# Output projection and second attention's projections as three products of split operands

## The chip, the cores and the metric

The kernel runs on one core of one Trainium2 chip. The metric is device microseconds of one execution; the median of several timed runs is quoted, and one further execution is profiled. Engines are named as in the profile: PE is TensorE's matrix products and PEld its weight loads, DVE is VectorE, ACT ScalarE, POOL GpSimd, SP SyncE. SPq and ACTq are the DMA issues of SyncE and ScalarE.

## The reference

A two-layer block on `x` of shape (8, 256, 512), fp32, cut to what matters here:

```
h   = causal depthwise conv of x (8 taps from cond, bias)
q, k, v = split(h @ qkv_w.T + qkv_b)                 # 16 heads of 32
a   = softmax(q k^T * scale + alibi bias, causal) v
x1  = x + (a @ out_w.T + out_b)                      # output projection
Q, K, V = einsum('oc,bct->bto', W, x1) for Wq, Wk, Wv  # 256 x 256 each, 16 heads of 16, 512 positions
y   = softmax((Q K^T / 4 + b) * m + (1 - m) * -1e30) V  # second attention, mask m = cond
out = x1 + ffn(y)                                    # gate, up, SiLU, down; weights rebuilt from control points
```

In the second attention the 256 rows of `x1` are the channels and the 512 columns are the positions.

## The kernel before, in words

Each engine has one program, written out by hand, with semaphores between them. Batch 0 is written separately, batches 1 to 6 are a loop, batch 7 stands behind the loop. The feed-forward of batch b - 1 runs inside batch b, and the first attention's projections and first scores of batch b + 1 run at the end of batch b. Batch 0 also rebuilds the down weights (gathered, split into a rounded high part and a low rest, and stored in DRAM) and the gate and up weights, eight chunks that GpSimd combines.

Within a batch TensorE goes through: exponent scores of the first attention and its value products (`values1`), the feed's first gate and up product, the output projection (L1101, eight products of 128x128x512 in the order of `PROJECTION`), the query and key projections of the second attention (L1112, eight products of 128x128x512), its values (L1120, eight of 128x128x256), then windows of score products (L1147) mixed with the feed, and 16 rounds of exponent scores (L1183) and value products (L1196).

VectorE divides each of four 256-column groups of the attention output by its row sums (reciprocal L838, product L840, result `o1`), then handles the feed's first gated product (L786) and its low rest (L790), then adds the projection to the residual, one 512-column half at a time (L849, result `x1`). ScalarE copies the projected queries out (L674); VectorE splits them (`split`, cast L770 and subtraction L772), multiplies the keys by the mask (L857), and splits those.

SyncE's queue is in order. After `x1_out` it stores `x1` in DRAM (L401), loads the residual of the feed's batch (L404), copies mask rows into the key stack (L432, four copies over all four groups), and then copies high and low parts into the query stack `q2` and key stack `k2`, group by group (`stacks2`, L425, twelve copies a group; the first score of a group waits for 192 counts, all twelve). Later come the next batch's residual and mask, and rows of maxima (`max_rows`, L332). `q2` and `k2` hold constant rows, written once in batch 0.

The output projection and the three projections of the second attention use plain fp32 operands. The scores and the down projection use operands bitcast to `float32r`; the down projection is already a sum of three such products, high by high, high by low and low by high (L1007, L1008, L1009).

Of the kernel before, what the change touches and what calls it, by code (L numbers as in the profile page):

```python
# [2 lines left out]

# [12 lines left out]
P = 128  # L16
# [27 lines left out]
ROWS2 = 64  # L44
# [76 lines left out]
def round_scores(k, i):  # L121
# [15 lines left out]
    "v2_ready": CT, "v2_out": CT, "aug_step": 3, "aug_high": 1, "aug_low": 1, "aug_rows": 64,  # L137
# [9 lines left out]
    "down_step": NT - 1, "sum_ready": LT, "sum_out": LT, "xr_loaded": 16, "out_stored": 16,  # L147
}
# [11 lines left out]
def block_program(nc, x_lanes, x_rows, taps, conv_b, qkv_wT, qk_b, v_b, out_wT, out_b, slopes, cond, w2T, att_b,  # L160
# [5 lines left out]
    key_dram = nc.dram_tensor("key_rows", (6, H1 * L), F32, kind="Internal").ap()  # L166
    alibi_dram = nc.dram_tensor("alibi_rows", (4, H1 * L), F32, kind="Internal").ap()
    with ExitStack() as ctx:
# [62 lines left out]

        halves = probs[:, 1].rearrange("p e n -> p (e n)")
# [29 lines left out]
        bias_loaded = sem("bias_loaded")  # L262
        big_loaded = sem("big_loaded")
        qk_loaded = [sem(f"qk_loaded{c}") for c in range(CT)]
# [37 lines left out]
        def _(sp):  # L302
# [57 lines left out]
            for i in range(2):  # L360
# [17 lines left out]
            stacks1(0)  # L378

# [9 lines left out]
            def batch(b, first=False, last=False):  # L389
# [51 lines left out]
                if not last:  # L441
# [4 lines left out]
                    wait("aug_rows", 64)  # L446
                    load_mask(cond[b])
# [125 lines left out]
        def _(act):  # L573
# [53 lines left out]
            def batch(b, first=False, last=False):  # L627
# [35 lines left out]
                if first:  # L663
                    for c in range(3, 5):
                        load_chunk(c)
# [814 lines left out]
```

## Time and profile before

| what | value |
|---|---|
| median of three timed runs | 1302.64 us |
| lowest, highest | 1294.46, 1304.24 us |
| the profiled execution | 1298.3 us |
| its span, first to last instruction | 1296.5 us |
| TensorE busy | 1192.3 us, 92% of the span |
| VectorE, ScalarE, GpSimd busy | 57%, 39%, 27% of the span |
| mean granted TensorE clock | 0.966 |

A busy share is an average over stages with different limits. Matrix products are pipelined and their modelled ends overlap, so the step of a chain of products is read from their starts. An fp32 product appears as two records, a `float32r` product as one.

### The profile page before, as it was taken

How to read it: one execution, taken by the hardware profiler on the slowest of the kernel's cores; microseconds unless marked ns; L12 is line 12 of the kernel's file. 1: busy time of each engine (PE TensorE's matmuls, PEld its weight loads, DVE VectorE, ACT ScalarE, POOL GpSimd, SP SyncE). 2: the span in 40 equal slices, each digit the busy share in tenths (PEclk: the TensorE clock that was granted, in tenths of full speed). 3: DMA queues.
4: the chain of work that ended last, by engine and by line, in shares of the span. 5: the costliest groups of instructions: out<-in, count | busy, mean ns of one | idle time of the engine just before them, and what ended most of it. 6: DMA issues, size and time to landing. Idle time of an engine off the chain costs nothing.

```text
span 1296.5 us, 20804 instructions
## 1 busy us (share of the span) xinstructions
PE 1192.3 (92%) x7400; PEld 682.4 (53%) x7400; DVE 743.9 (57%) x1173; ACT 501.4 (39%) x699; POOL 344.8 (27%) x201
## 2 busy tenths in 40 slices
PE   5685799999999999999999999999999999999988
PEld 4342245564555645565545645556455655556335
DVE  7666644558445773558535683557734684457812
ACT  1131244325532265224633256323643245322652
POOL 3283780092003800075000910047000830000000
PEclk9887679999999999999999999999999999999999
DMA  8989604382226704275134913267043732257024
GB/s 307 297 317 281 201 2 114 137 214 92 54 64 178 241 24 114 100 180 164 24 94 150 240 52 75 64 193 210 19 114 132 193 118 50 67 167 228 18 116 177
DMA packets 81057, 180.89 MB, mean 140 GB/s; under 512 B 14468, under 2 KB 54356, under 8 KB 71284
## 3 DMA queue, kind: packets, MB, share of 16 engines
q1 hardware_dynamic: 65104, 119.62, 33.2%
q10 hardware_dynamic: 14592, 55.86, 12.7%
q0 software_dynamic: 1280, 4.20, 0.9%
q8 instruction: 68, 1.11, 0.4%
q14 instruction: 13, 0.11, 0.0%
HBM read 106.41 MB, written 21.14 MB: 98 GB/s over the span
## 4 chain that ended last, share of the span: by engine, by line
PE 72%; DVE 8%; DMA 7%; POOL 5%; SPq 3%; issue 3%; ACT 2%; ACTq 0%; DVEq 0%; POOLq 0%
PE psum L1196 9%; PE psum L1147 8%; PE psum L967 8%; PE psum L1007 5%; PE psum L973 4%; PE psum L996 4%; PE psum L1009 4%; PE psum L1008 4%; PE psum L985 4%; PE psum L1101 4%; DVE max L868 4%; PE psum L1112 3%; PE psum L1183 3%; PE psum L1064 3%; SPq L425 3%
## 5 line engine op out<-in xcount | busy, mean ns | idle before, releaser
L868 DVE TENSOR_REDUCE max<-psum 128x1 f32<-128x512 f32 x512 | 326.2, 684 | 121.8 <-PE psum L1147 120.3
L705 ACT ACTIVATE probs<-psum 128x1024 f32<-128x1024 f32 x256 | 248.0, 1022 | 158.5 <-PE psum L1183 157.3
L1147 PE MATMUL psum<-k,q 52*128 52x512 f32 x512 | 198.1, 511 | 32.2 <-DMA k<-low 17.0
L555 POOL TENSOR_TENSOR h<-h_in,tap 128x1024 f32<-128x1024 f32 x7 | 13.3, 1897 | 611.9 <-DVE low L772 611.9
L1147 PEld LDWEIGHTS psum<-k,q 52*128 52x128 f32 x512 | 85.2, 194 | 160.3 <-DVE max L868 102.4
L1196 PE MATMUL psum<-probs,v 128*32 128x512 f32 x1024 | 140.7, 622 | 0.4 <-ACT probs L705 0.3
L1183 PE MATMUL psum<-q,k 54*128 54x512 f32 x512 | 113.8, 444 | 14.3 <-ACT probs L705 7.4
L565 POOL TENSOR_TENSOR h<-h,products 128x1024 f32<-128x1024 f32 x49 | 116.5, 2378 | 3.8
L1007 PE MATMUL psum<-stack 128*128 128x512 f32 x256 | 108.2, 423 | 0.0
L770 DVE CAST high<-low 128x1024 fp32r<-128x1024 f32 x32 | 24.9, 779 | 143.2 <-ACT low L586 115.4
L967 PE MATMUL psum<-h,qkv_w 128*128 128x256 f32 x448 | 103.5, 384 | 0.6 <-POOL h L565 0.6
L1008 PE MATMUL psum<-stack 128*128 128x512 f32 x256 | 100.7, 393 | 0.0
L1009 PE MATMUL psum<-stack 128*128 128x512 f32 x256 | 100.5, 393 | 0.0
L604 ACT ACTIVATE probs<-psum 128x512 f32<-128x512 f32 x64 | 38.2, 597 | 159.9 <-PE psum L996 159.9
L967 PEld LDWEIGHTS psum<-h,qkv_w 128*128 128x128 f32 x448 | 82.8, 190 | 28.5 <-issue 18.4
L562 POOL TENSOR_TENSOR products<-h_in,tap 128x1024 f32<-128x1024 f32 x49 | 93.2, 1903 | 3.3
L659 ACT ACTIVATE probs<-psum 128x768 f32<-128x768 f32 x64 | 48.9, 810 | 94.1 <-PE psum L1084 94.1
L838 DVE RECIPROCAL inv<-psum 128x256 f32<-128x256 f32 x32 | 56.2, 1758 | 46.3 <-PE psum L1064 45.5
L1183 PEld LDWEIGHTS psum<-q,k 54*128 54x128 f32 x512 | 53.9, 192 | 46.6 <-ACT probs L705 26.1
L973 PE MATMUL psum<-qkv_w,h 128*128 128x512 f32 x128 | 70.7, 674 | 2.7 <-issue 2.7
L996 PE MATMUL psum<-z,w_gate_up 64*128 64x256 f32 x512 | 68.3, 384 | 2.9 <-DVE stack L790 2.9
L815 DVE TENSOR_REDUCE max<-psum 128x2 f32<-128x256 f32 (+1 forms) x128 | 63.1, 552 | 13.5 <-PE psum L1035 12.8
(112 smaller groups left out, 1595.7 us busy)
## 6 DMA issues: line engine op xcount, KB each, us to landing
stack<-wd_sorted ACTq DMA_DIRECT2D x40, 1024.0 KB, 6.4
stack<-wd_sorted SPq DMA_DIRECT2D x24, 1024.0 KB, 6.9
stack<-high SPq DMA_DIRECT2D x128, 128.0 KB, 2.4
stack<-low SPq DMA_DIRECT2D x64, 128.0 KB, 2.4
q<-high SPq DMA_DIRECT2D x128, 64.0 KB, 4.0
k<-high SPq DMA_DIRECT2D x128, 64.0 KB, 4.1
h_in<-in_x_lanes SPq DMA_DIRECT2D x9, 512.0 KB, 4.0
x<-in_x_rows SPq DMA_DIRECT2D x8, 512.0 KB, 5.3
```

What stands on the lines that cost most here:

```text
L565: nc.gpsimd.tensor_tensor(h[:], h[:], products[:], ALU.add).then_inc(S["conv_step"], 1)
L705: nc.scalar.activation(probs[:, u // 2 % 2, u % 2 * 2:u % 2 * 2 + 2, :], psum[:, 2 + u % 2 * 2:4 + u % 2 * 2, :], ACT.Exp)\
L868: nc.vector.reduce_max(max2[:, g, e, i, t:t + 1], psum[:, bank, :], AX_X).then_inc(S["s2_max"], 1)
L967: last = nc.tensor.matmul(psum[:, o % 2, 0:L], qkv_w[:, c, o * P:(o + 1) * P], h[:, c, :], start=c == 0, stop=c == CT - 1)
L973: last = nc.tensor.matmul(psum[:, V1_BANKS[t], :], h[:, c, t * P:(t + 1) * P], qkv_w[:, c, 2 * D:3 * D], start=c == 0, stop=c == CT - 1)
L996: last = nc.tensor.matmul(psum[:, GU_BANK + g, u * L:(u + 1) * L], w_gu[rows, u, n, :], z[rows, n % 2, :], start=True, stop=True, skip_gro ...
L1007: nc.tensor.matmul(psum[:, SUM_BANK + s, :], r(inter_h[lhs]), r(w_h), start=n + g == 0, stop=False)
L1008: nc.tensor.matmul(psum[:, SUM_BANK + s, :], r(inter_h[lhs]), r(w_l), start=False, stop=False)
L1009: last = nc.tensor.matmul(psum[:, SUM_BANK + s, :], r(inter_l[lhs]), r(w_h), start=False, stop=n == NT - 1 and g == 1)
L1147: nc.tensor.matmul(psum[:, banks[s], :], r(q2[rows, g, i, t * P:(t + 1) * P]), r(k2[rows, g, i, :]), start=True, stop=True).then_inc(S["s2 ...
L1183: last = nc.tensor.matmul(psum[:, 2 + u % 2 * 2 + e, :], r(k2[rows, g, u % 2, kt * P:(kt + 1) * P]), r(q2[rows, g, u % 2, :]), start=True, ...
L1196: last = nc.tensor.matmul(psum[e * BLK:(e + 1) * BLK, 6, :], v2[:, t, head, :], probs[:, t % 2, e, :], start=t == 0, stop=t == CT - 1, ski ...
```

## The change

In batches 1 to 7 the output projection and the query, key and value projections become sums of three `float32r` products. For that, both sides are split into a rounded high part and a low rest.

- Weights: in batch 0 ScalarE makes the high parts of `out_w` and `w2` in `probs` and stores them in DRAM; VectorE subtracts them, so that `out_w` and `w2` then hold the low rests. Batch 0 itself still multiplies plain fp32. The plain weights first go from DRAM to DRAM and are loaded behind the first stacks.
- The high parts come back from DRAM in every batch but the last, for the next one: `out_w`'s (1 MB) into groups 0 and 1 of `q2` after 16 exponent scores, `w2`'s (0.75 MB) into groups 2 and 3 of `k2` after the last.
- `o1` is split group by group into `high`, `x1` half by half into groups 2 and 3 of `q2`.
- The constant and mask rows that this overwrites are written again in each batch, in two halves: groups 0 and 1 before `stacks2(0)`, groups 2 and 3 before `stacks2(2)`.
- The query and key projections are now ordered by `x1` half first, then query or key.

```diff
 # SyncE, start of the program
-            sp.dma_start(out_w[:], out_wT.rearrange("(c p) n -> p c n", p=P)).then_inc(big_loaded, 16)
-            sp.dma_start(w2[:].rearrange("p i c n -> p (i c) n"), w2T.rearrange("(m p) n -> p m n", p=P))\
-                .then_inc(big_loaded, 16)
+            sp.dma_start(plain_out, out_wT).then_inc(plain_copied, 16)
+            sp.dma_start(plain_w2, w2T).then_inc(plain_copied, 16)
...
             stacks1(0)
+            sp.wait_ge(plain_copied, 32)
+            sp.dma_start(out_w[:], plain_out.rearrange("(c p) n -> p c n", p=P)).then_inc(big_loaded, 16)
+            sp.dma_start(w2[:].rearrange("p i c n -> p (i c) n"), plain_w2.rearrange("(m p) n -> p m n", p=P))\
+                .then_inc(big_loaded, 16)
...
                 if not first:
                     wait("proj_ready", LT)
                     sp.dma_start(x_res, x1_dram[b - 1]).then_inc(S["xr_loaded"], 16)
+                    for e in range(2):
+                        row = e * ROWS2
+                        sp.dma_start(q2[row + ONE2:row + MAX2, 0:2, :, :].rearrange("p g i n -> p (g i n)"),
+                                     key_dram[2:6, 0:2 * 2 * D]).then_inc(S["refixed"], 16)
...
+                def mask_rows2(g):
+                    for e in range(2):
+                        for i, part in enumerate((aug_h, aug_f)):
+                            row = e * ROWS2 + ONE2 + 2 * i
+                            sp.dma_start(k2[row:row + 2, g:g + 2, :, :].rearrange("p g i n -> p (g i) n"),
+                                         part[:, None, :].broadcast_to([2, 4, D])).then_inc(S["aug_rows2" if g else "aug_rows"], 16)
...
                 wait("aug_low", 1)
-                for e in range(2):
-                    for i, part in enumerate((aug_h, aug_f)):
-                        row = e * ROWS2 + ONE2 + 2 * i
-                        sp.dma_start(k2[row:row + 2, :, :, :].rearrange("p g i n -> p (g i) n"),
-                                     part[:, None, :].broadcast_to([2, NG * 2, D])).then_inc(S["aug_rows"], 16)
+                mask_rows2(0)
                 for g in range(NG):
+                    if g == 2:
+                        wait("v2_ready", CT)
+                        if not first:
+                            for e in range(2):
+                                row = e * ROWS2
+                                sp.dma_start(q2[row + ONE2:row + MAX2, 2:4, :, :].rearrange("p g i n -> p (g i n)"),
+                                             key_dram[2:6, 0:2 * 2 * D]).then_inc(S["refixed2"], 16)
+                                sp.dma_start(k2[row + MAX2:row + END2, 2:4, :, :].rearrange("p g i n -> p (g i n)"),
+                                             key_dram[2:4, 0:2 * 2 * D]).then_inc(S["refixed2"], 16)
+                        mask_rows2(2)
                     stacks2(g)
...
                 for g in range(1, NG):
                     max_rows(b, g)
+                if first:
+                    sp.wait_ge(high_stored, 32)
                 if not last:
+                    wait("t2_ready", 2 * 2 * CT)
+                    sp.dma_start(out_high_flat, high_out).then_inc(S["out_high"], 16)
                     stacks1(b + 1)
                     wait("conv_step", 2 * TAPS)
                     sp.dma_start(h_in[:, :, TAPS - 1:], x_lanes[b + 1]).then_inc(S["x_loaded"], 16)
+                    wait("t2_ready", NP)
+                    sp.dma_start(w2_high_flat, high_w2).then_inc(S["w2_high"], 16)
 # ScalarE, batch 0, behind load_chunk(3) and (4)
+                    wait("pv1_ready", CT)
+                    act.wait_ge(big_loaded, 32)
+                    for made, plain in zip(made_high, (out_flat, w2_flat)):
+                        nc.scalar.activation(r(made), plain, ACT.Copy).then_inc(weights_high, 1)
+                    for i, store in enumerate((high_out, high_w2)):
+                        act.wait_ge(weights_high, i + 1)
+                        act.dma_start(store, made_high[i]).then_inc(high_stored, 16)
 # VectorE, batches 1 to 7, per group of o1 (x1 likewise per half: add, cast, subtract)
+                    nc.vector.tensor_tensor(inv1[:], psum[:, 6 + g % 2, 0:L], inv1[:], ALU.mult)\
+                        .then_inc(S["o1_made"], 1)
+                    dve.wait_ge(S["o1_made"], fed(b, "o1_made", g + 1))
+                    nc.vector.tensor_copy(r(o1_h[:, g, :]), inv1[:]).then_inc(S["o1_high"], 1)
+                    dve.wait_ge(S["o1_high"], fed(b, "o1_high", g + 1))
+                    nc.vector.tensor_tensor(r(o1_l[:, g, :]), inv1[:], o1_h[:, g, :], ALU.subtract)\
                         .then_inc(S["o1_out"], 1)
 # VectorE, batch 0, behind the key split
+                if first:
+                    wait("v2_ready", CT)
+                    for i, plain in enumerate((out_flat, w2_flat)):
+                        dve.wait_ge(weights_high, i + 1)
+                        nc.vector.tensor_tensor(r(plain), plain, made_high[i], ALU.subtract).then_inc(weights_low, 1)
 # TensorE
+            def three_terms(out, stat_h, stat_l, moving_h, moving_l, start, stop):
+                nc.tensor.matmul(out, r(stat_h), r(moving_h), start=start, stop=False, skip_group_check=True)
+                nc.tensor.matmul(out, r(stat_h), r(moving_l), start=False, stop=False, skip_group_check=True)
+                return nc.tensor.matmul(out, r(stat_l), r(moving_h), start=False, stop=stop, skip_group_check=True)
...
+                for t, i in product(range(LT), range(2)) if not first else ((0, 0), (1, 0), (0, 1), (1, 1)):
...
+                            last = three_terms(psum[:, banks[o], :], w2_h[:, i, t, rows], w2[:, i, t, rows],
+                                               x1_h[:, t, :], x1_l[:, t, :], t == 0, t == LT - 1)
...
                     if n == 0:
                         wait(f"stack2_{g}", 192)
-                        if g == 0:
-                            wait("aug_rows", 64)
+                        if g % 2 == 0:
+                            wait("aug_rows2" if g else "aug_rows", 64)
+                            if not first and g:
+                                pe.wait_ge(S["refixed2"], fed(b, "refixed2", 64))
+                            elif not first:
+                                pe.wait_ge(S["refixed"], fed(b, "refixed", 32))
```

## Rows read from the trace of the kernel before

**Rows 1.** The page's chain that ended last, shares by engine.

```profile
PE 72%; DVE 8%; DMA 7%; POOL 5%; SPq 3%; issue 3%; ACT 2%; ACTq 0%; DVEq 0%; POOLq 0%
```

**Rows 2.** That chain in order of time, batch 3: start us, us, what.

```profile
538.17 0.24 PE psum L1081 x2
...
550.12 6.88 PE psum L1112 x16
...
558.48 1.24 DVE low L772
...
564.02 2.33 DMA k<-low
```

**Rows 3.** TensorE's timeline at batch 3's first score: start, duration, line, idle before.

```profile
566.57 0.50 PE L1147 MATMUL psum<-k,q 52*128 52x512 f32 x2 [0.26 <-DMA k<-low]
```

**Rows 4.** Group by line on TensorE: shapes, count, busy us, mean ns, idle before.

```profile
L1120 PE MATMUL psum<-w,x 128*128 128x256 f32 x128 | 28.9, 379 | 0.0
```

**Rows 5.** TensorE's timeline in a down projection: second and last of its twelve products.

```profile
563.63 0.40 PE L1008 MATMUL psum<-stack 128*128 128x512 f32 x1
...
565.92 0.39 PE L1009 MATMUL psum<-stack 128*128 128x512 f32 x1
```

**Rows 6.** VectorE's timeline in batch 3, attention output to query split.

```profile
540.76 1.76 DVE L838 RECIPROCAL inv<-psum 128x256 f32<-128x256 f32 x1 [0.87 <-PE psum L1064]
...
543.08 1.76 DVE L838 RECIPROCAL inv<-psum 128x256 f32<-128x256 f32 x1
544.87 0.42 DVE L840 TENSOR_TENSOR o<-psum,inv 128x256 f32<-128x256 f32 x1
...
550.16 0.69 DVE L849 TENSOR_TENSOR x<-psum,x 128x512 f32<-128x512 f32 x1 [1.88 <-PE psum L1101]
554.29 0.69 DVE L770 CAST high<-low 128x1024 fp32r<-128x1024 f32 x1 [3.44 <-ACT low L674]
555.02 1.23 DVE L772 TENSOR_TENSOR low<-low,high 128x1024 f32<-128x1024 f32 x1
```

**Rows 7.** SyncE's queue in batch 3, `x1` store to the first group's stacks.

```profile
551.02 0.36 SPq L401 DMA_DIRECT2D x_scratch<-x  x1
551.58 0.35 SPq L404 DMA_DIRECT2D o<-x_scratch  x1
...
554.11 1.29 SPq L432 DMA_DIRECT2D k<-aug_f  x1
555.54 4.00 SPq L425 DMA_DIRECT2D q<-high  x4
...
563.38 1.22 SPq L425 DMA_DIRECT2D k<-low  x2
```

**Rows 8.** Timelines: SyncE's last issues of the first maxima rows; their first use.

```profile
594.94 1.30 SPq L332 DMA_DIRECT2D q<-max_l  x2
...
602.12 0.40 PE L1183 MATMUL psum<-q,k 54*128 54x512 f32 x2
```

**Rows 9.** SyncE queue's own waits: us in total, times, longest us.

```profile
SPq L321 <- DVE high L770: 75.1, 14, 9.0
```

**Rows 10.** The chain in order of time in batch 0.

```profile
49.00 10.52 DMA wd_natural<-w_gate_up
...
185.07 3.69 PE psum L967 x16
```

**Rows 11.** Busy time by window, two stretches of batch 0: last three, clock, DMA share, GB/s.

```profile
50.00:60.00 10.00, 8.65 (x32) 4.82 (x30) 5.62 (x11) 0.00 (x0) 0.20 (x1) 0.81 0.89 318
...
90.00:100.00 10.00, 10.00 (x25) 4.39 (x24) 3.69 (x5) 0.93 (x2) 6.76 (x8) 1.00 1.04 378
```

**Rows 12.** The same view, a stretch at the end of batch 2.

```profile
526.00:528.00 2.00, 2.00 (x3) 0.72 (x3) 0.00 (x0) 0.00 (x0) 0.00 (x0) 0.50 0.07 16
```

**Rows 13.** The chain in order of time, the same product in two batches.

```profile
524.60 5.13 PE psum L973 x8
...
974.91 3.44 PE psum L973 x8
```

More of the change, by code:

```diff
@@ L2 @@
 from contextlib import ExitStack
+from itertools import product
 import concourse.bass as bass
@@ L446, in batch @@
                     wait("aug_rows", 64)
+                    wait("aug_rows2", 64)
                     load_mask(cond[b])
@@ L704, in batch @@
                         act.wait_ge(S["inter_low"], fed(b, "inter_low", NT))
+                    if j == 0 and first:
+                        act.wait_ge(high_stored, 32)
+                        act.wait_ge(weights_low, 2)
                     nc.scalar.activation(probs[:, u // 2 % 2, u % 2 * 2:u % 2 * 2 + 2, :],
@@ L848, in batch @@
                     wait("proj_ready", t + 1)
+                    if first:
+                        nc.vector.tensor_tensor(x1[:, t, :], psum[:, t, :], x1[:, t, :], ALU.add)\
+                            .then_inc(S["x1_out"], 1)
+                        continue
                     nc.vector.tensor_tensor(x1[:, t, :], psum[:, t, :], x1[:, t, :], ALU.add)\
+                        .then_inc(S["x1_made"], 1)
+                    dve.wait_ge(S["x1_made"], fed(b, "x1_made", t + 1))
+                    nc.vector.tensor_copy(r(x1_h[:, t, :]), x1[:, t, :]).then_inc(S["x1_high"], 1)
+                    dve.wait_ge(S["x1_high"], fed(b, "x1_high", t + 1))
+                    nc.vector.tensor_tensor(r(x1_l[:, t, :]), x1[:, t, :], x1_h[:, t, :], ALU.subtract)\
                         .then_inc(S["x1_out"], 1)
@@ L1100, in batch @@
                         wait("o1_out", c + 1)
-                    last = nc.tensor.matmul(psum[:, t, :], o1[:, c, t * P:(t + 1) * P], out_w[:, c, :],
-                                            start=c == 0, stop=c == CT - 1, skip_group_check=True)
+                    rows = slice(t * P, (t + 1) * P)
+                    if first:
+                        last = nc.tensor.matmul(psum[:, t, :], o1[:, c, rows], out_w[:, c, :],
+                                                start=c == 0, stop=c == CT - 1, skip_group_check=True)
+                    else:
+                        last = three_terms(psum[:, t, :], o1_h[:, c, rows], o1_l[:, c, rows],
+                                           out_h[:, c, :], out_w[:, c, :], c == 0, c == CT - 1)
                     if c == CT - 1:
@@ L1106, in batch @@
                 wait("p1_out", H1 // 2)
-                for i, (banks, ready) in enumerate(((Q2_BANKS, "q2_ready"), (K2_BANKS, "k2_ready"))):
-                    for t in range(LT):
-                        if i == 0:
-                            wait("x1_out", t + 1)
-                        for o in range(LT):
-                            last = nc.tensor.matmul(psum[:, banks[o], :], w2[:, i, t, o * P:(o + 1) * P],
-                                                    x1[:, t, :], start=t == 0, stop=t == LT - 1, skip_group_check=True)
-                            if t == LT - 1:
-                                last.then_inc(S[ready], 1)
+                if not first:
+                    pe.wait_ge(S["w2_high"], fed(b, "w2_high", 16))
+                for t, i in product(range(LT), range(2)) if not first else ((0, 0), (1, 0), (0, 1), (1, 1)):
+                    banks, ready = ((Q2_BANKS, "q2_ready"), (K2_BANKS, "k2_ready"))[i]
+                    if i == 0:
+                        wait("x1_out", t + 1)
+                    for o in range(LT):
+                        rows = slice(o * P, (o + 1) * P)
+                        if first:
+                            last = nc.tensor.matmul(psum[:, banks[o], :], w2[:, i, t, rows], x1[:, t, :],
+                                                    start=t == 0, stop=t == LT - 1, skip_group_check=True)
+                        else:
+                            last = three_terms(psum[:, banks[o], :], w2_h[:, i, t, rows], w2[:, i, t, rows],
+                                               x1_h[:, t, :], x1_l[:, t, :], t == 0, t == LT - 1)
+                        if t == LT - 1:
+                            last.then_inc(S[ready], 1)
                 for n in range(CT):
```

37 lines of the change are left out of this document (32 added, 5 removed).

## The prediction

> **What bounds the kernel now.** I read three views in turn. First the shares of the chain that ended last: TensorE holds 72% of it, VectorE 8%, DMA 7%, SyncE's queue 3% [rows 1]. So most microseconds taken from TensorE shorten the kernel, provided nothing else waits at the same place. Second, the chain in order of time around the changed stage of one steady batch (batch 3, 536 to 570 us; the other loop batches repeat it). TensorE's projections come first, then a VectorE split, then SyncE's copies, and the last link is 2.33 us of a copy into the key stack, landing at 566.34 [rows 2]. Third, the timeline shows the first score of the second attention starting at 566.57, after only 0.26 us idle on that copy [rows 3]. Thus two chains arrive together there: TensorE's own work, and the path x1, split, SyncE, stack. A shorter TensorE alone gains a quarter of a microsecond per batch. From that score on TensorE has hardly a gap to the batch's end, so the start of that score is what I compute. The change acts in batches 1 to 7; batch 0 only prepares weights.
>
> **TensorE's part.** One true fp32 product 128x128x512 is two records; 16 records take 6.88 us for the query and key projections [rows 2], 0.86 us a product. The split product already in the kernel, the down projection, runs from 563.63 to 565.92 in ten steps [rows 5], 0.229 us a step; three make 0.69 us. The output projection and query/key have 8 products each: 16 x 0.17 = 2.7 us saved. The values have 8 products of 256 columns: now 128 records for 8 batches, 28.9 us [rows 4], 3.6 us a batch; two consecutive split steps of 256 columns take 0.24 us [rows 2], so 24 x 0.12 = 2.9 us, 0.7 saved. In all 3.4 us a batch, 24 us in seven, if nothing else were paced.
>
> **VectorE's part, on the path.** Each 256-column group of the attention output now costs a reciprocal (1.76) and a product (0.42) [rows 6]. Added are a cast to the high part and a subtraction. The cast of 1024 columns takes 0.69 and the subtraction of 1024 takes 1.23 [rows 6]; scaled with a start of about 0.15 us (estimate from the product of 256 at 0.42 and the add of 512 at 0.69), 256 columns take about 0.28 and 0.41. Group 2's reciprocal starts at 540.76 [rows 6] because TensorE delivers then. Groups 2 and 3 then take about 3.0 each instead of 2.25, so group 3 is finished at 546.8 rather than 545.3. TensorE, faster now, gets to that group about 0.6 us before and waits. Behind it on VectorE are queued the feed's gated product and remainder, with a ScalarE cast between them, about 2.1 us: 549.0. Then x1 is made twice: add 0.69, cast 0.42, subtract 0.69 with gaps, 1.87 each. x1_out's first count is due at 550.85, the second at 552.7. Before, the second add ended at 550.85 [rows 6]. **x1 is 1.9 us later**, though its projection was shortened. TensorE idles some 1.2 us before the second projections, which then end about 0.5 us earlier than now; it would arrive at the first score near 565.3.
>
> The query split is 1.8 us later too: TensorE's 18 steps from 550.9 and a fill end at 555.4, and with ScalarE's copy the cast starts at 556.1 instead of 554.29 [rows 6]. The key products queue behind it on VectorE: the key's low part is ready near 561.5, against 558.48 + 1.24 = 559.72 [rows 2]. The new order of the query and key loops recovers nothing here, as the query's second half now stands behind the key's first.
>
> **SyncE's part, on the path.** SyncE's queue stores x1 at 551.02, loads the residual, issues four mask-row copies, then the stacks. The fourth mask copy takes 1.29 us, the first four query copies 4.00, against 1.22 for two afterwards [rows 7]: the four end at 559.54, so with two free issues of 0.61 at their end the queue is held up until about 558.3, 7.2 us behind the x1 store's issue. With x1 1.9 later the same queue starts at 552.9, and two constant-row copies are added before the masks; these are halved in bytes, not in number. Bounds for the first score. Below: no hold-up at all, query copies from 556.9, twelve issues of about 0.62 us and the same landing give 566.1, that is minus 0.3 (VectorE's parts allow it). Above: the hold-up shifts with x1 and two issues move from inside it to behind it, 1.9 + 1.1 = plus 3.0. I take plus 1.8, since the hold-up in these rows stands at a fixed distance from the x1 store.
>
> The Trainium skill (DMA: Bandwidth & Descriptors, "Why a DMA increments its semaphore by 16 and not by 1") says that a copy is spread over as many DMA engines as divide its outermost dimension. By it, two-partition mask rows use two engines, and halving them would shorten the hold-up; as an estimate by that page the shift would be nearer 1.3 us and the total near 1316. The slow fourth mask issue agrees with slow draining, but cannot tell which engines drained.
>
> The other eight added issues (constant rows and mask rows of groups 2 and 3) precede the stacks of those groups and push SyncE's later work by roughly 4 us with the shift above. Who waits: the first group's maxima rows, whose last issue pair ends at 594.94 + 1.30 = 596.24, needed by TensorE at 602.12 [rows 8]. Nearly all of that cover goes; I take 0, with up to 2 us a batch if it is short. The two streams of high weights follow quiet places in SyncE's queue: it waits 75.1 us over 14 waits for VectorE's casts at the first stacks [rows 9]. I take 0; without that cover one issue costs about 0.35 [rows 7]. The added semaphore waits on TensorE protect buffers freed long before, except the x1 and stack waits already counted.
>
> **Batch 0.** Its chain runs through DMA: a 1 MB store from 49.00 takes 10.52 us on it, and after further loads and GpSimd's convolution TensorE's work on the next batch enters it at 185.07 [rows 10]. DMA share is 0.89 at 318 GB/s and 1.04 at 378 GB/s in two stretches of it [rows 11]. The change adds a second load of 1.84 MB behind the first stacks (5.8 us at 318) and a store of the same size from ScalarE's queue (4.9 at 378). Before these sit two casts of about 1.9 and 1.4 us on ScalarE, and two subtractions on VectorE, about 4.3 or more, ahead of its sorts; TensorE's scores wait for both engines. Bounds: 2 us (the casts, if the copies fill holes) to 14 (all in sequence). I take 8, as the shares show few holes.
>
> **Sum.** Seven batches at 1.8 = 12.6, plus 8 = 20.6. The profiled execution took 1298.3 us (span 1296.5), so 1318.9. The median is 1302.64, 4.3 higher; the three timed runs lie on both sides of the profiled one. I say 1320.
>
> **Rivals.** (B) The clock falls as well. TensorE would wait some 2.5 to 3 us at the first score. In this trace the granted clock was 0.50 in 526 to 528, after a stretch in which TensorE had short waits [rows 12]; that is the 1.2 GHz level, full is 2.4. Eight records there took 5.13 us, and 3.44 in the like place of a later batch [rows 13], so 1.7 us. Once per batch: 12 more, 1331. Against it: no row shows a fall at the first score, where the wait now is 0.26 us [rows 3]. The Trainium skill (TensorE: Matmul & The Clock Gate, Part 1) likewise has two clock states and a fall after idleness.
>
> (C) Not slower: SyncE's hold-up is set by the data of the mask rows, not by x1. Then the first score comes 0.3 to 1.0 us earlier, the latter being TensorE's own arrival; seven batches give minus 2 to 7, batch 0 adds 2 to 8: 1293 to 1304, say 1300. It decides if the query copies start without a pause after the cast. For it: the slow issues are the fourth mask copy and those right behind it [rows 7]. Against: VectorE's order leaves the key's low part 1.8 us later anyway.
>
> (D) Faster: VectorE's added parts hide, and TensorE's 3.4 us come through in full: 1298.3 - 24 + 2 = 1276. For it: 72% of the chain [rows 1]. Against: VectorE is in order and runs group 2 and 3 back to back [rows 6]. That the change doesn't speed TensorE at all (three split products as long as one) would add to A only where TensorE is last, so it stays within A's range.
>
> **How the numbers follow.** A 0.52, B 0.17, C 0.21, D 0.10. The range 1296 to 1340 takes in A's bounds but for the last few microseconds of their worst sum (12.6 replaced by 21, 8 by 14, giving 1333, and 1340 with a late maxima row), B, and most of C; D stays out. Within 1%, about what a measurement of this kernel can tell from no change, is 1289.6 to 1315.7: most of C and a third of A. Faster takes D and a little of C.
>
> **What would show it.** In the profile after: split products at 0.23 us a step; x1's store 1.5 to 2 us later against the start of the output projection; TensorE idle 2 us or more before the first score with the key copy as releaser; batch 0's first TensorE work on the next batch near 193 instead of 185. Wrong if that idle time is under 0.5 us, or if the query copies follow the cast with no held issue.

## The result, and the profile after

The changed kernel took 1318.93 us (median of 4 runs, 1316.87 to 1319.84) against 1302.52 us of the kernel before beside it: a ratio of 1.0121, 95% interval 1.0088 to 1.0154. Timed once more, it took 1313.95 us, ratio 1.0088 (1.0055 to 1.0121). The change makes the kernel about 1% slower, 11 to 16 us. The profiled span is 1318.0 us, 21.5 us longer than before, with a mean granted clock of 0.953 against 0.966.

The page's chain of the changed kernel, shares by engine, answers to [rows 1]: TensorE fell from 72% to 56%, VectorE doubled, SyncE's queue went from 3% to 11%.

```profile
PE 56%; DVE 16%; SPq 11%; DMA 7%; issue 4%; ACT 3%; ACTq 1%; POOL 1%; DVEq 0%; POOLq 0%
```

Now the changed stage of batch 3. TensorE's timeline (start, duration, line, idle before in brackets):

```profile
564.16 0.50 PE L1044 MATMUL psum<-q,high 128*128 128x512 f32 x1 [0.70 <-DVE high L906]
...
567.91 0.50 PE L1044 MATMUL psum<-q,k 128*128 128x512 f32 x1 [0.73 <-DVE q L924]
...
573.55 0.28 PE L1044 MATMUL psum<-k,q 128*128 128x256 f32 x1
573.67 0.28 PE L1045 MATMUL psum<-w,q 128*128 128x256 f32 x1
...
584.11 0.50 PE L1254 MATMUL psum<-k,q 52*128 52x512 f32 x2 [1.65 <-DMA k<-low]
```

The 24 query and key products run from 567.91 to 573.55, 5.64 us where the fp32 ones took 6.88 [rows 2]; a value step is 0.12 us. By its steps TensorE does save the 3.4 us, and the brackets show where they went: 0.70 us of waiting for o1's low part, 0.73 for x1's, and 1.65 at the first score, where 0.26 stood before [rows 3].

VectorE's timeline of the same batch, beside [rows 6]:

```profile
561.10 1.76 DVE L895 RECIPROCAL inv<-psum 128x256 f32<-128x256 f32 x1
562.89 0.42 DVE L901 TENSOR_TENSOR inv<-psum,inv 128x256 f32<-128x256 f32 x1
563.35 0.29 DVE L904 CAST high<-inv 128x256 fp32r<-128x256 f32 x1
563.68 0.43 DVE L906 TENSOR_TENSOR high<-inv,high 128x256 fp32r<-128x256 f32 x1
...
568.95 0.69 DVE L924 TENSOR_TENSOR q<-x,q 128x512 fp32r<-128x512 f32 x1
573.07 0.69 DVE L827 CAST high<-low 128x1024 fp32r<-128x1024 f32 x1 [3.43 <-ACT low L728]
```

To compare batches I count from the transpose that turns the first attention's maxima (524.32 before, 541.50 after). The last group of o1 is finished 22.61 us behind it instead of 20.97, x1 28.14 instead of 26.53, the query cast starts 31.57 instead of 29.97: everything on VectorE is 1.6 us later. Then SyncE's queue, beside [rows 7]:

```profile
569.84 0.36 SPq L424 DMA_DIRECT2D x_scratch<-x  x1
...
573.89 0.62 SPq L459 DMA_DIRECT2D k<-aug_f  x1
574.64 2.46 SPq L452 DMA_DIRECT2D q<-high  x4
...
580.95 1.22 SPq L452 DMA_DIRECT2D k<-low  x2
```

The fourth mask copy takes 0.62 us instead of 1.29 and the first four query copies 2.46 instead of 4.00: **the hold-up is gone**, though the copies still start 0.9 us behind the end of the cast, because SyncE is issuing mask rows until then. So SyncE gives back what VectorE lost, and the first score stands 42.61 us behind the transpose instead of 42.25.

The first maxima rows still come in time, with less to spare: their last issues end at 616.95, and TensorE uses them at 619.62, 2.7 us later, where 5.9 us lay between before [rows 8].

```profile
615.64 1.31 SPq L352 DMA_DIRECT2D q<-max_l  x2
...
619.62 0.41 PE L1290 MATMUL psum<-q,k 54*128 54x512 f32 x2
```

Where, then, are the 21.5 us? TensorE's timeline gives the opening of each batch. Batch 0's transpose is 3.0 us later, batch 0 itself is 9.95 us longer (170.98 against 161.03), and batches 1 to 7 are 8.6 us longer in all, +0.65, +3.59, +0.31, +0.90, -1.23, +4.77 and -0.40. The loop's loss is thus in two batches, 2 and 6, not in each. About 1.7 us of batch 6 only changed places: the clock fell at the opening of batch 5 before and at that of batch 6 after, which is also batch 5's -1.23. In batches 2 and 6, TensorE waited for down weights. The first line is from its list of waits (total us, times, longest), the next two are the waits of batch 2 in its timeline, and then come SyncE's issues of the two streams of high weights in that batch.

```profile
PE psum L1092 <- DMA stack<-wd_sorted: 3.8, 5, 1.1
...
455.97 0.50 PE L1092 MATMUL psum<-stack 128*128 128x512 f32 x1 [1.07 <-DMA stack<-wd_sorted]
...
461.44 0.50 PE L1092 MATMUL psum<-stack 128*128 128x512 f32 x1 [0.75 <-DMA stack<-wd_sorted]
...
502.39 0.35 SPq L508 DMA_DIRECT2D q<-high_out  x1
...
529.82 0.55 SPq L513 DMA_DIRECT2D k<-high_w  x1
```

The view by windows (after the busy times: clock, DMA share, GB/s) has the same stretch of batch 2, 51.35 us behind the transpose, in the kernel before:

```profile
426.41:446.41 20.00, 20.00 (x128) 14.03 (x127) 13.98 (x25) 4.78 (x9) 19.08 (x10) 1.00 0.97 304
```

and in the changed kernel, with the fall of the clock behind it:

```profile
440.00:460.00 20.00, 18.93 (x124) 13.20 (x122) 12.68 (x22) 4.22 (x9) 18.70 (x9) 1.00 0.99 274
...
476.00:478.00 2.00, 1.92 (x12) 0.34 (x9) 2.00 (x4) 1.94 (x2) 0.00 (x0) 0.75 0.05 13
478.00:480.00 2.00, 2.00 (x10) 1.15 (x7) 0.70 (x2) 0.02 (x1) 0.00 (x0) 0.50 0.04 8
```

The DMA engines are full from 440 to 460, but they were so before (0.99 and 0.97), and no weights came late then. Now two weight loads come 1.07 and 0.75 us late, and some 15 us later the clock is at 0.50, the 1.2 GHz level that [rows 12] showed at another place. Batch 6 repeats it (0.80 and 0.77 us, then the clock). The streams of high weights are issued some 40 us after these waits, and those of the batch before some 75 us ahead of them, so they do not bring them on. What does is not shown.

In batch 0 the chain in order of time now goes through ScalarE's queue and VectorE's subtractions and reaches the next batch's first product at 198.24 instead of 185.07 [rows 10]:

```profile
93.40 4.23 ACTq L695
97.73 3.29 ACT probs L716 x2
101.03 3.27 ACTq L719
104.33 4.91 ACTq L719
...
117.55 3.35 DVE out_w L940
120.90 2.20 DVE w L940
...
198.24 3.46 PE psum L1052 x16
```

### The profile page after: what moved, and what is told of

Its sections match the earlier page's. It is cut to its first block, busy times and chain, and to the rows that moved or that the text cites. A ratio compares the mean times of both kernels' runs of the same rounds, so it can differ in the third digit from the quotient of the medians.

```text
span 1318.0 us, 21393 instructions
## 1 busy us (share of the span) xinstructions
PE 1181.7 (90%) x7568; PEld 703.7 (53%) x7568; DVE 783.0 (59%) x1259; ACT 505.3 (38%) x701; POOL 347.3 (26%) x201
## 4 chain that ended last, share of the span: by engine, by line
PE 56%; DVE 16%; SPq 11%; DMA 7%; issue 4%; ACT 3%; ACTq 1%; POOL 1%; DVEq 0%; POOLq 0%
PE psum L1303 9%; PE psum L1052 8%; PE psum L1254 8%; SPq L452 7%; PE psum L1058 4%; DVE max L948 4%; PE psum L1092 4%; PE psum L1290 3%; DVE inv L895 3%; PE psum L1070 3%; PE psum L1093 3%; PE psum L1094 3%; PE psum L1081 2%; DMA stack<-wd_sorted 2%; SPq L459 2%
## 5 line engine op out<-in xcount | busy, mean ns | idle before, releaser
L1092 PE MATMUL psum<-stack 128*128 128x512 f32 x256 | 107.8, 421 | 3.8 <-DMA stack<-wd_sorted 3.8
L658 ACT ACTIVATE stack<-psum 128x512 fp32r<-128x512 f32 x64 | 38.3, 599 | 88.7 <-DVE psum L843 78.4
```

Source lines behind the costliest of these rows:

```text
L1092: nc.tensor.matmul(psum[:, SUM_BANK + s, :], r(inter_h[lhs]), r(w_h), start=n + g == 0, stop=False)
```

## The experiments

Theory: (1) in the loop, SyncE's in-order issues behind x1 set the first score, and VectorE's splits of o1 and x1 push x1 back; (2) in batch 0, making the high weights costs 8 us or more. The way of the plain weights, first from DRAM to DRAM and then loaded late, is called the detour. Rivals: the loss is all in batch 0, or all in the number of added copies. Each run was timed against the kernel before on the same chip. One profile is one draw: batch 0 of the changed kernel took 170.98 us in one and 163.77 in another. So verdicts go by the ratios, and the profiles by what repeats in each batch.

| run | median us | ratio | 95% interval | batch 1 opens | mean first score, batches 1 to 6 | mean from there to the batch's end |
|---|---|---|---|---|---|---|
| before | 1302.52 | 1 | | 226.40 | 41.66 | 107.84 |
| after | 1318.93 | 1.0121 | 1.0088 to 1.0154 | 239.34 | 41.98 | 109.03 |
| after, again | 1313.95 | 1.0088 | 1.0055 to 1.0121 | 232.55 | 41.92 | 109.21 |
| weights only | 1308.97 | 1.0034 | 1.0009 to 1.0058 | 237.47 | 42.12 | 108.83 |
| no weights | 1314.32 | 1.0069 | 1.0045 to 1.0093 | 234.92 | 42.18 | 109.81 |
| detour only | 1306.41 | 1.0033 | 1.0017 to 1.0049 | 234.20 | 41.57 | 108.38 |
| masks halved | 1303.04 | 0.9997 | 0.9970 to 1.0025 | 225.20 | 41.80 | 108.10 |
| SyncE's order | 1312.26 | 1.0062 | 1.0036 to 1.0089 | 234.48 | 41.03 | 109.40 |
| two queues | 1302.75 | 0.9997 | 0.9975 to 1.0018 | 233.47 | 40.41 | 110.02 |
| QKV only | 1301.39 | 0.9983 | 0.9960 to 1.0007 | 233.91 | 40.34 | 108.82 |
| output only | 1306.76 | 1.0013 | 0.9988 to 1.0038 | 234.37 | 42.36 | 108.28 |
| output, no split | 1304.00 | 1.0014 | 0.9991 to 1.0037 | 232.53 | 41.26 | 108.30 |
| QKV, two queues | 1296.68 | 0.9963 | 0.9937 to 0.9989 | 235.57 | 39.69 | 109.14 |
| QKV, late weights | 1298.46 | 0.9958 | 0.9931 to 0.9986 | 233.90 | 39.93 | 108.95 |

The last three columns come from TensorE's timeline of the profiled run: the transpose that opens batch 1; the first score's start, counted from its batch's transpose; and the time from there to the next transpose. In every profile at least one of the six batches takes 107.76 to 107.99 us for that last stretch, so about 107.8 is what it takes undisturbed, and what lies above is waits and clock. The profiled runs of after, weights only, no weights, detour only, output only and QKV, late weights are the slowest of their series, so their columns are high. The first score's place carries the clock too: where the clock fell at a batch's opening (batches 3 to 5 of the kernel before) it comes about 1.2 us later. Between batches with the same clock, after differs from before by 0.3 to 0.4 us, and QKV only by -0.8 to -1.0.

**Batch 0: weights only, no weights, detour only.** Three runs take batch 0's work apart. The first adds to the kernel before all of the change's weight preparation, and multiplies as before. The second takes casts, stores and subtractions out of the changed kernel (the weights are then not split: plain weights stand as both parts). The third adds to the kernel before only the detour.

```diff
 # detour only, on the kernel before
-            sp.dma_start(out_w[:], out_wT...).then_inc(big_loaded, 16)
-            sp.dma_start(w2[:]..., w2T...).then_inc(big_loaded, 16)
+            sp.dma_start(plain_out, out_wT).then_inc(plain_copied, 16)
+            sp.dma_start(plain_w2, w2T).then_inc(plain_copied, 16)
...
             stacks1(0)
+            sp.wait_ge(plain_copied, 32)
+            sp.dma_start(out_w[:], plain_out...).then_inc(big_loaded, 16)
+            sp.dma_start(w2[:]..., plain_w2...).then_inc(big_loaded, 16)
```

> The kernel before with batch 0's preparation alone: detour and late load of the weights, casts, stores of the high parts, subtractions. Later batches multiply plain fp32 with the low rests, so their output is left out of account; their work is that of before. Theory (batch 0 carries most of the loss): batch 0 grows by 13 us, as in the changed kernel (there batch 1's turn of the maxima comes at 239.3 instead of 226.4), later batches stay, total 1302.5 + 13 = 1315. Rival (the preparation is hidden and the later batches lose the time): at most 4 us more, 1302 to 1306.

> The changed kernel without casts, stores and subtractions in batch 0; the detour and late load stay, and the per-batch streams carry the plain weights, so the products are wrong by that and their work is the same. Theory: the turn of batch 0's maxima stays 3 us late (detour), the other 10 us of batch 0 go, total 1319 - 10 = 1309. Rival (the detour and late load alone delay batch 0's loads): no more than 3 us less, 1316 to 1319.

> The kernel before with nothing of the change but the way of the plain weights: copied from DRAM to DRAM at the start and loaded behind the first stacks; no casts, stores or subtractions. Theory (the copy and the late load are batch 0's cost, since all kernels with them open batch 1 at 232.5 to 239 us and the two without at 225 and 226): 1307 to 1310 us, batch 1 opens at 232 or later. Rival (the casts, held stores and subtractions are the cost): 1302 to 1305 us, batch 1 opens at 228 or earlier.

The preparation in all costs 0.34%, 4.4 us, between theory and rival. The detour alone costs 0.33%, the same, at 1306.41 us just below the range that I gave its theory and above the rival's; batch 1 opens at 234.20, as the theory had it. So casts, stores and subtractions add nothing measurable to the kernel before; the intervals would show some 4 us. Taking them out of the changed kernel gives 0.52% or 0.19%, by which of its two timings one takes; the intervals overlap with both, so for that kernel 0 to about 7 us stay open. How the detour costs 4 us is suggested by the chain of its profile, batch 0:

```profile
90.91 20.54 DMA z_table<-in_gu_points
...
118.54 20.85 DMA z_table<-in_gu_points
...
156.41 1.86 POOL h L561
...
191.19 5.38 PE psum L973 x16
```

The chain of the kernel before has one such long load where this one has two:

```profile
110.58 22.84 DMA z_table<-in_gu_points
...
138.60 7.14 DMA z_table<-in_gu_points
...
150.32 1.86 POOL h L555
```

And the view by windows, from 130 to 140 us, the kernel before first and then detour only:

```profile
130.00:140.00 10.00, 7.63 (x15) 3.25 (x14) 9.83 (x18) 0.00 (x0) 4.34 (x3) 0.50 0.78 273
```

```profile
130.00:140.00 10.00, 9.71 (x18) 4.51 (x17) 9.97 (x19) 0.00 (x0) 0.55 (x1) 0.50 1.02 377
```

The DMA engines are full for longer (share 1.02 instead of 0.78 in that stretch), and the second load takes 20.85 us. GpSimd's chunks, of which each waits for such a load, end later, its convolution starts at 156.41 where it started at 150.32 before, and TensorE's first product of the next batch stands at 191.19 instead of 185.07. All twelve profiles with the detour open batch 1 at 232.5 or later, the two without at 226.4 or earlier. Five of the twelve, the runs on one half of the change, have only one of the two weights on the detour and open batch 1 no earlier than the others, so the delay does not go with the detour's bytes alone.

**Masks halved.** The kernel before, with only its mask rows written in two halves.

```diff
-                               part[:, None, :].broadcast_to([2, NG * 2, D])).then_inc(S["aug_rows"], 16)
+                               part[:, None, :].broadcast_to([2, 4, D])).then_inc(S["aug_rows2" if g else "aug_rows"], 16)
...
+                mask_rows2(0)
                 for g in range(NG):
+                    if g == 2:
+                        mask_rows2(2)
```

> The kernel before with its mask rows written in two halves, groups 0 and 1 ahead of the first stacks, groups 2 and 3 ahead of the third. Theory (the hold-up in SyncE's queue comes from the bytes of the mask rows): the first four query copies take 2.5 us instead of 4.0 and the first score waits for TensorE alone, 0.26 us earlier a batch, total 1300 to 1303. Rival (the hold-up comes from the x1 store and residual load in front): 4.0 stays, and the first score stays at its place.

SyncE's queue in batch 3 of this run, and of the run with whole mask rows but no split of x1 (output only, below):

```profile
553.27 0.62 SPq L432 DMA_DIRECT2D k<-aug_f  x1
554.17 2.47 SPq L425 DMA_DIRECT2D q<-high  x4
```

```profile
564.18 1.02 SPq L458 DMA_DIRECT2D k<-aug_f  x1
565.33 3.95 SPq L451 DMA_DIRECT2D q<-high  x4
```

Halved rows: no hold-up. Whole rows: hold-up, 3.95 us. **The hold-up is the mask rows' bytes**, as rival C said, and no fixed distance from the x1 store. By the Trainium skill (DMA: Bandwidth & Descriptors, "Why a DMA increments its semaphore by 16 and not by 1") a copy uses as many engines, up to 16, as divide its slowest dimension, which is two for these rows. The runs agree with the direction, shorter rows and no hold-up, and show no engines. The time didn't move, within 0.27%: the first score waits for nothing here, TensorE itself arrives then.

**SyncE's order, then two queues.** The changed kernel with the first groups' masks and constant rows moved ahead of the wait for x1, and the x1 store behind the first group's stacks. Then, in addition, the four low-part copies of that group from ScalarE's queue, and the residual load behind the weight loads.

```diff
 # SyncE's order
+                    wait("aug_low", 1)
+                    mask_rows2(0)
                     wait("proj_ready", LT)
...
                 for g in range(NG):
+                    if not first and g == 1:
+                        store_x1()
 # two queues: ScalarE
+            def low_rows2(b, off, stack, blocks):
+                act.wait_ge(S["low2"], at(b, "low2", 1 + off // 1024))
...
+                        act.dma_start(stack[row:row + DH, 0, :, :].rearrange("p t n -> p (t n)"),
+                                      low[e * DH:(e + 1) * DH, off:off + 1024]).then_inc(S["stack2_0"], 16)
```

> The changed kernel with SyncE's order changed: the first mask and constant rows go ahead of the wait for x1, the x1 store and residual load behind the first group's stacks. Theory (the first score is set by SyncE's queue behind x1): the first query copy starts when its cast ends, 0.85 us earlier; TensorE's wait at the first score falls from 1.65 to 0.8; total 1319 - 6 = 1313. Rival (VectorE's split sets it): first score unmoved, 1319. A second rival: the two moved copies of 512 KB collide with the down weights, whose waits grow, 1319 to 1325.

> The changed kernel with SyncE's new order (the first groups' constant and mask rows ahead of the x1 store, the store behind the first group's stacks), the residual load moved up behind the weight loads, and the four copies of low parts of the first group issued from ScalarE's queue. Theory (behind x1 it is SyncE's in-order issues, some 0.62 us each, that set the first score and the first maxima rows): the idle time ahead of the first score, 0.75 to 0.94 us with the new order alone, goes to 0.3 or less; the maxima rows' last issues come some 3 us earlier, so the idle on them (0.8 to 2.0 us in three batches) goes too; 1302 to 1305 us against 1312 with the new order alone. Rival (the rest of the loss sits in VectorE's splits of o1 and x1): the idle goes but shows up elsewhere in the batch, 1310 to 1313 us.

> The changed kernel once more, unaltered, to stand on the same chip beside the kernels that follow and to show how far its batches scatter. Both theories: about 1319 us.

The new order brings the first score 0.95 us earlier on average (41.98 to 41.03), with 0.90 us of idle time ahead of it instead of 1.69, as the theory said; the time, 1312.26, is the theory's too, but its interval overlaps with both of the changed kernel's. Something else is late at once: in four batches of the loop TensorE waits for the first maxima rows, longest in batch 3.

```profile
612.41 0.51 PE L1300 MATMUL psum<-q,k 54*128 54x512 f32 x2 [2.03 <-DMA q<-max_l]
```

With two queues that wait is down to 0.23 us, in batch 3 alone of the loop, and the one at the first score to 0.24 there. Here are ScalarE's issues, and TensorE at the first score:

```profile
566.19 1.22 ACTq L680 DMA_DIRECT2D q<-low  x2
...
567.85 1.41 ACTq L680 DMA_DIRECT2D k<-low  x2
```

```profile
572.30 0.50 PE L1276 MATMUL psum<-k,q 52*128 52x512 f32 x2 [0.24 <-DMA k<-high]
```

The time is that of the kernel before, ratio 0.9997 against 1.0088 on the same chip: 11.2 us between the medians, for the place at which twelve copies are queued. This is the theory's number, and it is not the clock's doing: over all timed runs the mean granted clock is 0.957 here and 0.956 in the changed kernel. Part of the gain is given back, though, in the profile, which is 6 us above the median: the stretch behind the first score is 110.02 us instead of 107.84. In batches 2 to 6 the clock was at 0.50 for 3 to 14 us, from some 5 to 10 us behind the first exponent score on. Adding up (1 - granted clock) over windows of 2 us, batches 1 to 6 lost 5.1 us before, 8.5 and 10.4 in the two profiles of the changed kernel, and 22.2 here. But masks halved, as fast as the kernel before, lost 8.6, so that 5.1 is a low draw. What lets the clock fall there is left open.

**The two halves.** QKV only drops the output projection's split, its stream, its constant rows and the preparation of its weights; output only drops the other, with whole mask rows again.

```diff
 # QKV only: VectorE and TensorE as in batch 0
-                    if first:
+                    if True:
                         nc.vector.tensor_tensor(o1[:, g, :], psum[:, 6 + g % 2, 0:L], inv1[:], ALU.mult)\
...
-                    if first:
+                    if True:
                         last = nc.tensor.matmul(psum[:, t, :], o1[:, c, rows], out_w[:, c, :],
 # output only: the same edits at x1 and at w2's products
```

> Only the second attention's projections as three products; the output projection in plain fp32 with o1 as before, no stream of its high weights, no constant rows written again for groups 0 and 1. Theory (the cost sits where x1 becomes late, through o1's splits on VectorE, and in the held SyncE queue, which the halved mask rows relieve): about 3 us in batch 0, 0 to 0.7 us a batch in the loop, 1306 to 1310 us, less than the other half. Rival (the cost is the number of added copies, eight more a batch here against two in the other half): 1313 to 1316 us, more than the other half.

> Only the output projection as three products; x1 and the second attention's projections in plain fp32, the mask rows whole as in the kernel before, constant rows written again only for groups 0 and 1. Theory: o1's splits make x1 about 0.8 us later, the hold-up of the whole mask rows is back and two issues are added, about 1.2 to 1.5 us a batch, and about 4 us in batch 0: 1312 to 1317 us. Rival (the number of added copies decides, and here it is two a batch): 1305 to 1308 us.

QKV only is no slower than the kernel before although it carries the detour of `w2`, and faster than I expected: the first score is 1.3 us earlier, 0.8 to 1.0 where the clock is the same. Output only is at the rival's number, and its first score is 0.7 us later, the hold-up of the whole mask rows included. The halves don't add: -0.17% and +0.13% alone, +0.9 to +1.2% together. What they share is one chain, and that it explains the sum was not tested by itself: o1's splits make x1 late, x1's splits make it later, and behind x1 stands SyncE.

**Output, no split.** To see what o1's splits cost, VectorE writes its product straight as the high part.

```diff
-                    nc.vector.tensor_tensor(inv1[:], psum[:, 6 + g % 2, 0:L], inv1[:], ALU.mult)\
...
-                    nc.vector.tensor_copy(r(o1_h[:, g, :]), inv1[:]).then_inc(S["o1_high"], 1)
...
-                    nc.vector.tensor_tensor(r(o1_l[:, g, :]), inv1[:], o1_h[:, g, :], ALU.subtract)\
+                    nc.vector.tensor_tensor(r(o1_h[:, g, :]), psum[:, 6 + g % 2, 0:L], inv1[:], ALU.mult)
```

> As the kernel with only the output projection split, but VectorE writes its product straight as the high part; the cast and the subtraction of o1 are left out, and what stands in the rows of the low part is old (so the third product multiplies stale data). Theory (the output projection's half gains nothing because VectorE's splits of o1 push x1 back): x1 about 1 to 1.5 us earlier in each batch, the idle ahead of the projection (0.7 us) gone, the first score 0.8 to 1.2 us earlier, 1298 to 1301 us against 1306.8 with the splits. Rival (the stream of high weights, the constant rows written again and batch 0 take the gain): 1305 to 1308 us.

VectorE now waits 0.87 us for TensorE at the second and third group. The cast and the subtraction had filled that wait; at the fourth group, where there is none, they come on top.

```profile
547.08 1.76 DVE L881 RECIPROCAL inv<-psum 128x256 f32<-128x256 f32 x1 [0.87 <-PE psum L1130]
548.88 0.42 DVE L887 TENSOR_TENSOR high<-psum,inv 128x256 fp32r<-128x256 f32 x1
```

In batch 1, where the clock fell in neither run, x1's store is issued 23.74 us behind the transpose instead of 24.96 and the first score comes at 40.22 instead of 41.45, 1.2 us earlier, as the theory said. But the time did not follow: 1.0014 against 1.0013, the rival's side (medians 1304.00 and 1306.76). With intervals of 0.25% to each side, 7 us should have been seen. So o1's splits are on the path of the first score, but not the whole reason why this half gains nothing. One profile of each, of which one is the slowest of its series, can't tell where the 1.2 us a batch went. The clocks of all timed runs tell more: over twelve runs each, the mean granted clock is 0.964 with the splits and 0.958 without. (1 - clock) times the span is then 47 and 55 us, against 49 and 48 in the kernel before beside them. **So the run without splits lost about 8 us more to the clock**, which is what seven batches of 1.2 us would have gained. This is an account and not a proof, since some of that clock fell where TensorE waited anyway. QKV only shows the like: 56 us against 49.

**QKV with two queues, and with late weights.** The half that gains, with the queue of the run above; then also with w2's high part made in batch 0's rounds of exponent scores, in `high`.

```diff
 # late weights: ScalarE, batch 0, in the rounds
+                    if first and j == LATE:
...
+                        nc.scalar.activation(r(high[:, 0:3 * LT * L]), w2_flat, ACT.Copy).then_inc(weights_high, 1)
+                        act.wait_ge(weights_high, 1)
+                        act.dma_start(high_w2, high[:, 0:3 * LT * L]).then_inc(high_stored, 16)
```

> Only the second attention's projections as three products, and SyncE's new order with the first group's low parts issued from ScalarE's queue (x1's store and the residual load behind the first group's stacks). Theory (the 1.2 to 1.5 us of idle time ahead of the first score are SyncE's issues behind x1 and can be taken away): the idle goes to 0.3 us or less, the batches become about 1.2 us shorter each, 1292 to 1296 us. Rival (VectorE's split of x1 sets the first score): the idle stays over 0.8 us, 1299 to 1302 us.

> As the kernel with only the second attention's projections split and the two queues, but in batch 0 the high part of w2 is made, stored and subtracted in the rounds of exponent scores, in the scratch that held the first stacks' high parts, not ahead of the second projections; the copy from DRAM to DRAM and the late load stay. Theory (the cost in batch 0 is the casts, held stores and subtractions in the stretch in which the DMA engines are full): 2 to 4 us below the kernel without this move. Rival (the cost is the copy from DRAM to DRAM and the late load): the same time within 1 us.

Both beat both kernels: 0.9963 and 0.9958, 5 us under the kernel before. The idle time before the first score, 1.30 us on average with one queue, is 0.55, between theory and rival. Moving the casts showed no gain (1298.46 against 1296.68 us), the rival's case and in keeping with the detour run, though intervals of 0.27% do not exclude the 2 us that the theory asked for at least.

## Why the prediction came out right

The total was right, 1320 against 1318.93, and this was luck. The loop lost 8.6 us in the profile where I had 12.6, and batch 0 with its opening 13.0 where I had 8, so that two errors cancel; the second timing, 1313.95, is 6 us lower.

- **TensorE's saving** was right to the step: 0.23 and 0.12 us, 3.4 us a batch, nearly all of it turned into waits.
- **VectorE's delay** was slightly high: x1 1.6 us later, not 1.9.
- **SyncE's part failed**: "I take plus 1.8, since the hold-up in these rows stands at a fixed distance from the x1 store." It stands on the mask rows' bytes, and the change halves them. The query copies followed without a held issue, which I had named as what would prove me wrong; the idle time ahead of the first score was 1.65 us, not 2 or more. The first score came 0.3 us later on average (41.66 to 41.98), nearer to my lower bound of minus 0.3 than to plus 1.8, and seven batches give under 3 us, not 12.6. The sentence on the Trainium skill's page, with 1.3 us, leaned the right way and was still too much.
- **What the loop lost in its place**: 8.6 us in the profile, of which the first scores explain about 2.6 (batches 1 to 7, 0.37 on average) and the stretch behind them 6.0. By kind, 3.8 of it are waits for down weights and about 3.4 the clock (8.5 us lost in batches 1 to 6 instead of 5.1). I had that clock as rival B, at the wrong place. Single profiles can't lay either on the change. TensorE's waits for down weights were 3.8 and 3.3 us in the two profiles of the whole change, 0 in the kernel before and with two queues, but also 1.0 with masks halved and 0.9 in the detour run, neither of which has a stream, and 2.3 and 3.2 in the two kernels that beat the kernel before; so they don't decide the time. The clock has more behind it: over all timed runs its mean was 0.954 and 0.956 in the changed kernel, 0.962 in the kernel before beside the second. (1 - clock) times the span is 61 and 58 us against 49, so up to 9 to 12 us are the clock's, less what fell where TensorE waited anyway, as in batch 0. The two queues, at a clock as low as the changed kernel's, took the 11 us away all the same, which is the whole loss against the kernel before, with the detour's 4.3 us still in it.
- **The maxima rows**, whose lateness I took at 0, did come in time, with 2.7 us to spare; that was gone as soon as the first score came earlier: 2.03 us of waiting with SyncE's new order.
- **Batch 0** was sized right, 8 with bounds 2 to 14, for 9.95 in one profile (and 3.0 more ahead of its transpose); its make-up was wrong. I summed loads, casts, stores and subtractions. The measured price is the detour's, 4.3 us, and 0 to 7 us for the rest. In this profile the chain went through the casts and stores; in most others it went through GpSimd.

Rival C was right about SyncE's hold-up and wrong about the time. It had the first score 0.3 to 1.0 us earlier, and it came 0.3 later, behind VectorE's later x1 and the issues that still stood in front of the query copies; and it left the waits and the clock behind the first score at nothing.

## What to carry to other kernels

When a transfer is late behind an in-order queue, first ask whether it is held by bytes in front of it or by its own issue: a split into smaller copies, or a second queue, tells at once. A saving on the busiest engine is worth what the chain of its operands leaves: here the half behind o1 gained 0.4% once its copies left the crowded queue, and the half with o1's splits gained nothing, and nothing either when the splits were left out. An earlier start may be given back by the clock, so compare the granted clock of all timed runs before you explain a gain that didn't come. And in a preparation stage look first at what the DMA engines are full with, not only at the instructions that one sees.

## What the runs showed of the hardware

- The same four copies took 4.00 or 3.95 us behind four two-partition copies of 16 KB a partition, and 2.46 or 2.47 behind copies of half the size.
- Copying 1.84 MB from DRAM to DRAM and loading it again cost 4.3 us although `out_w` had landed more than 25 us before its first use. In the profile the DMA engines were full for longer (share 1.02 instead of 0.78 from 130 to 140 us), and a later load on the chain took 20.85 us.
- The granted clock fell to 0.50 in different batches from profile to profile of one kernel. Batches 1 to 6 of the changed kernel lost 8.5 us to it in one and 10.4 in the other. Over twelve timed runs each, output only had a mean granted clock of 0.964, and 0.958 when VectorE's splits were left out and x1 came 1.2 us earlier.
